# ScalarE's step functions in the second attention, moved behind the second head's turned probabilities and the values

## The reference

```
x = layernorm(x + L0_attn(x));  x = layernorm(x + L0_ffn(x))
x = layernorm(x + L1_attn(x));  x = layernorm(x + L1_ffn(x))
# L1_attn: causal attention, batch 4, 256 tokens, 32 heads of 128, with rotated
#          queries and keys (rope), plus a second, latent branch of 32 heads
# L1_ffn:  weights rounded to 16 levels (NF4) in blocks of 64 before their use:
absmax = max(|w|) per block;  idx = searchsorted(bounds, w / absmax)
w_used = NF4_CODE[idx] * absmax
```

## Time and profile before

| | |
|---|---|
| time, median of 3 runs (lowest, highest) | 2439.47 us (2437.63, 2440.76) |
| the profiled execution: its time; its span | 2439.4 us; 2437.5 us |
| busy in the span: PE, DVE, POOL, ACT | 2246.6, 1797.1, 1577.7, 1433.7 us |
| the second attention | about 805 to 2200 us of the span |
| one of its middle groups | about 173 us |

### The profile page before, as it was taken

How to read it: one execution, slowest core, us unless ns; L and a number is a source line. 1 busy time by engine, 2 the same in 40 slices (tenths; PEclk the granted TensorE clock), 3 DMA queues, 4 the chain that set the end, 5 groups by cost and what they waited for, 6 DMA issues and landing times. The chain is left out here.

```text
span 2437.5 us, 43787 instructions
## 1 busy us (share of the span) xinstructions
PE 2246.6 (92%) x14144; PEld 1993.3 (82%) x14144; DVE 1797.1 (74%) x3270; ACT 1433.7 (59%) x3947; POOL 1577.7 (65%) x1336
## 2 busy tenths in 40 slices
PE   7899999988998899998999999999999999987998
PEld 5788988876886788887888888888888888876886
DVE  5788777767533798888887888888888888964322
ACT  2657676652332567676676676776776766663232
POOL 3556657413444778778878878878788788752343
PEclk8999999988999999999999999999999999998999
DMA  3201111000001101101101111111111011004000
GB/s 101 63 27 42 59 32 43 11 18 1 1 1 55 56 25 54 54 13 61 51 25 50 47 33 51 39 42 50 40 40 52 31 50 40 19 5 146 1 18 18
DMA packets 49555, 95.38 MB, mean 39 GB/s; under 512 B 6768, under 2 KB 14224, under 8 KB 48976
## 3 DMA queue, kind: packets, MB, share of 16 engines
q1 hardware_dynamic: 49296, 92.24, 12.2%
HBM read 81.47 MB, written 10.75 MB: 38 GB/s over the span
## 5 line engine op out<-in xcount | busy, mean ns | idle before, releaser
L1280 POOL TENSOR_TENSOR a_nf_acc<-a_nf_acc,a_nf_term 128x512 f32<-128x512 f32 (+1 forms) x416 | 592.4, 1424 | 142.6 <-ACT a_nf_term L1374 72.0
L1334 ACT ACTIVATE a_probs<-bank,a_dip 128x128 f32<-128x128 f32 (+1 forms) x512 | 208.7, 420 | 192.1 <-DVE a_dip L1615 192.1
L1343 ACT ACTIVATE a_probs<-a_probs,a_share 128x128 f32<-128x128 f32 (+1 forms) x512 | 192.4, 464 | 67.7 <-DVE a_share L1621 67.7
L1799 POOL TENSOR_TENSOR f_w_lo<-WGU,f_w_hi 128x512 fp32r<-128x512 f32 x88 | 112.7, 1302 | 175.0 <-ACT f_w_hi L1810 175.0
L1261 POOL TENSOR_TENSOR a_qk_lo<-a_straight,a_qk_hi 128x512 fp32r<-128x512 f32 (+1 forms) x160 | 193.4, 1211 | 41.3 <-ACT a_qk_hi L1320 41.3
L64 PE MATMUL bank<-a_wo_hi,a_ot_hi 128*128 128x512 f32 x512 | 212.3, 415 | 0.0
L1626 DVE TENSOR_TENSOR a_pt_lo<-bank,a_pt_hi 128x384 fp32r<-128x384 f32 x256 | 141.0, 551 | 91.1 <-ACT a_pt_hi L1351 90.4
L1320 ACT ACTIVATE a_qk_hi<-a_straight 128x512 fp32r<-128x512 f32 (+1 forms) x160 | 94.4, 590 | 184.3 <-DVE a_straight L1600 184.3
L66 PE MATMUL bank<-a_wo_hi,a_ot_lo 128*128 128x512 f32 x512 | 201.2, 393 | 0.0
L65 PE MATMUL bank<-a_wo_lo,a_ot_hi 128*128 128x512 f32 x512 | 200.9, 392 | 0.0
L1685 DVE TENSOR_SCALAR a_nf_term<-a_nf_unit 128x512 f32<-128x512 f32 (+1 forms) x288 | 193.5, 716 | 3.4 <-DVE a_nf_unit L1668 0.6
(11 more groups left out here) (242 smaller groups left out, 8468.0 us busy)
## 6 DMA issues: line engine op xcount, KB each, us to landing
a_raw<-in_l_o SPq DMA_DIRECT2D x64, 256.0 KB, 2.8
a_raw<-in_l_vk SPq DMA_DIRECT2D x32, 384.0 KB, 3.1
a_raw<-in_l_ql SPq DMA_DIRECT2D x32, 320.0 KB, 2.9
a_raw<-in_l_ou SPq DMA_DIRECT2D x32, 288.0 KB, 2.8
a_raw<-in_l_nr SPq DMA_DIRECT2D x16, 384.0 KB, 3.1
a_nf_raw<-in_w_nf SPq DMA_DIRECT2D x24, 256.0 KB, 2.6
coded_w<-a_nf_acc SPq DMA_DIRECT2D x24, 256.0 KB, 2.0
f_codes<-coded_w SPq DMA_DIRECT2D x6, 512.0 KB, 3.9
```

Source lines behind the costliest of these rows:

```text
L1280: pool.tensor_tensor(acc, left, nf_term[:, i % CODE_RING, 0:w], ALU.add).then_inc(nf_added, 1)
L1334: act.activation(probs[:, n % 2, col:col + keys], bank[:, at:at + keys], ACT.Exp, bias=dip[:, n % 2, i:i + 1], accum_out=total[:, n % 2, i ...
L1343: ins = act.activation(cell, cell, ACT.Copy, scale=share[:, n % 2, i:i + 1])
L1799: pool.tensor_tensor(lo, src, hi.bitcast(F32), ALU.subtract).then_inc(part_lo[i], 1)
```

## The change

ACT's order within a step of the second attention: `code_terms(n)` goes behind `probs_high(n-1, 1)` and behind the high part of the values (VL), and stays ahead of the high parts of rotated queries (A) and keys (K). Nothing is computed differently, and no other engine's program is touched.

```diff
                     shares_applied(n)
-                    code_terms(n)
                     if not (first and n < 1):
                         probs_high(n - 1, 1)
-                    for name in l1_step_units(n, last):
-                        unit_high(name)
+                    units = l1_step_units(n, last)
+                    for name in units:
+                        if name[0] == "VL":
+                            plain_high(name)
+                    code_terms(n)
+                    for name in units:
+                        if name[0] != "VL":
+                            rope_high(name)
```

## The result

| | before | changed |
|---|---|---|
| median of 4 runs, us | 2440.09 | 2531.53 |
| range, us | 2437.63 to 2440.76 | 2529.29 to 2532.35 |
| profiled span, us | 2437.5 | 2530.5 |
| mean granted clock of TensorE | 0.969 | 0.954 |

The changed kernel takes 91.4 us more: the ratio is 1.0375, with a 95% interval of 1.0357 to 1.0393. The forecast was 2549, from 2485 to 2592.

A forecast was written before the change was run, and what follows sets the result against it. PE was taken to set the pace, busy 161.9 of 173 us in a middle group. Shifts of 76 us (56 within groups, 20 at passages) plus 33 us of clock on 2439.4 gave 2549 us, range 2485 to 2592.

The forecast's parts named there:

- The closed chain: PE's second turn, ACT's terms, POOL's sums, DVE's end and start of a piece, PE's second turn: closed, without slack.
- No slack, at the ends that do not look so: Read in step 8: L1648 starts at 1236.90, POOL's last sum ends at 1236.87, so a later sum delays it.
- Step 7 into 8: Piece's end in step 8: POOL's sum 2.2 us later behind the values' wait, taken as 2.0 us a group.
- Step 10 into 11: Piece's end in step 11, behind two VL: POOL's sum and PE's turn 4.5 us later in each group.
- the rival of half the shift: Sums run faster away from DVE's work, POOL has other gaps, the copies' lead helps: 2475 us, chance 10%.
- Step 11 into 0: Passage to the next group: sum 4.2 us later, POOL's gap in step 12 absorbs 1.3, leaving 2.9 us.
- Step 0 to 5: Piece's end in step 5: sum 1.8 us later, POOL's 1.30 us gap in step 1 takes most, leaving 0.5 us.
- The tail, costed at nothing: DVE's gain from copies 0.3 to 0.8 us sooner was costed at nothing, as given back at each piece's end.
- The clock: 22 falls at 1.5 us, 33 us: Behind longer PE stalls in steps 0, 5, 8 and 11: 22 additional falls to 1.2 GHz, 33 us, bounds nothing to 55.
- DVE's lead given back: DVE's waits for copies of turned probabilities and values halve, but at each piece's end it waits for POOL instead.
- Rotated queries with 0.4 us to spare: Rotated queries come 2 to 4 us later; tightest place, step 14, has some 0.4 us spare; charged nothing.
- the rival in which the clock holds: POOL's shift comes, but the low clock falls into the stalls and costs nothing: 2515 us, chance 17%.

The follow-up runs named there:

- The kernel with the clock kept: Changed kernel with zero-adding matmuls keeping PE busy ahead of the second turn in steps 0, 5, 8 and 11: 2495.74 us.
- its last link cut: Kernel before with DVE's L1648 moved to the end of steps 0, 5, 8 and 11: 2426.38 us; with the whole change added: 2438.76 us.
- the other order of DVE: Kernel before, DVE taking shares and first low halves ahead of a piece's end and start: 2500.83 us; with the change added: 2504.03 us.
- The run with the old order ahead of the ends: Changed kernel with ACT's old order kept in steps 0, 7, 10 and 11, new order in the others: 2458.35 us, ratio 1.0082 to the kernel before.
- The run with the new order in the tail alone: Kernel before with ACT's new order only in steps 12 to 15 of the last group: 2433.80 us, ratio 0.9972.

## Why the prediction was right, step by step

The kernel with the clock kept allows the sum to be read term by term, since its stretches hold the shifts and hardly any low clock. Differences to before, summed over the groups, in us:

| term | predicted shift | measured, clock kept | changed kernel, clock and all |
|---|---|---|---|
| step 5 to 8 | 16 | 15.7 | 21.1 |
| step 8 to 11 | 36 | 27.2 | 39.1 |
| step 11 to 0 | 20 | 18.7 | 25.3 |
| step 0 to 5 | 4 | 1.9 | 14.5 |
| tail | none | -5.4 | -8.3 |

*The closed chain.* Right, and the runs show it as the cause: with its last link cut, the change costs 12 us (3 on the other order of DVE). That it had no slack was read off two numbers that nearly met, the end of POOL's sum and the start of L1648; the list of waits did not name it. The new order in two steps alone cost 57 us; the forecast's two shifts are 8 × (2.0 + 4.5) = 52, and the stretches gave 45 with 11 from the clock.

*No slack, at the ends that do not look so.* The prediction read this in step 8 and took it for all ends. In steps 11 and 0 of the kernel before, L1648 starts 1.07 and 0.77 us behind POOL's last sum, and it is shorter:

```profile
1267.94 1.30 POOL L1280 TENSOR_TENSOR a_nf_acc<-a_nf_acc,a_nf_term 128x512 f32<-128x512 f32 x1 [0.18 <-POOL a_nf_acc L1280]
1269.19 1.30 POOL L1261 TENSOR_TENSOR a_qk_lo<-a_straight,a_qk_hi 128x512 fp32r<-128x512 f32 x1
...
1270.31 0.72 DVE L1648 SCALAR_TENSOR_TENSOR a_nf_acc<-a_nf_acc,a_nf_top 128x512 f32<-128x512 f32 x1
...
1152.61 1.28 POOL L1261 TENSOR_TENSOR a_qk_lo<-a_straight,a_qk_hi 128x512 fp32r<-128x512 f32 x1
...
1153.43 1.08 DVE L1648 SCALAR_TENSOR_TENSOR a_nf_acc<-a_nf_acc,a_nf_top 128x576 f32<-128x576 f32 x1
```

In step 11 it ends at 1271.03, in step 0 at 1154.51: 0.54 and 0.62 us behind the end of POOL's subtraction, as in step 8 (0.54). Gap and duration make 1.79, 1.85 and 1.79 us. So its end is tied to POOL's stream and not to its own start, and the later sum moves it by the full shift there too. In the changed kernel all 31 ends that wait start 0.02 to 0.04 us behind the sum and take 1.75 to 1.80 us. Without this, step 11's shift would have been a good us smaller. The prediction named the port and put its worth at a few tenths of a us at most. That these two ends have no slack it did not read from their rows, so there the forecast was right partly by luck.

*Step 7 into 8: 2.0 us.* Measured 34.67 - 32.83 = 1.84 in the groups in which the clock did not fall ahead of it. In the others it was 36.8, so 4.0.

*Step 10 into 11: 4.5 us, with a clock fall 6.0.* This is the term that was too big. Measured 3.8 with the clock kept (36.15 for 32.37 in a middle group; 27.2 over the eight groups), 4.0 in the middle groups with the new order in steps 7 and 10 alone, and 4.8 in the changed kernel with one low stretch. POOL's sum indeed waits for ACT (it starts at 1302.79), but the way behind it became shorter:

```profile
1300.27 0.44 ACT L1324 ACTIVATE a_vl_hi<-bank 128x320 fp32r<-128x320 f32 x1 [1.73 <-PE bank L66]
1300.60 1.32 ACT L1368 ACTIVATE a_nf_term<-a_nf_unit,a_edges 128x512 f32<-128x512 f32 x2
...
1302.79 1.30 POOL L1280 TENSOR_TENSOR a_nf_acc<-a_nf_acc,a_nf_term 128x512 f32<-128x512 f32 x1 [3.69 <-ACT a_nf_term L1374]
...
1305.58 1.77 DVE L1653 SCALAR_TENSOR_TENSOR a_nf_acc<-a_nf_acc,a_nf_top 128x512 f32<-128x512 f32 x1 [2.54 <-POOL a_nf_acc L1280]
```

The sum takes 1.30 us and not 1.62; DVE stands still beside most of it. From ACT's copy of the values to the sum's start it is 2.52 us, where the prediction had 0.44 + 2.21 = 2.65. Those are 0.45 us. The other 0.3 lie ahead of it: with the clock kept, PE ends the second VL 29.01 us behind the end of the piece in step 8 (1286.47 - 1257.46), and before 29.30 (1267.96 - 1238.66). The prediction took off such a gain of PE in step 7 and not here. The rival of half the shift had named the shorter sum, and was right on its sign.

*Step 11 into 0: 2.9 us.* Measured 18.7 / 7 = 2.7 with the clock kept. The gap of POOL that absorbs part of it was read rightly.

*Step 0 to 5: 0.5 us.* Measured 1.9 / 7 = 0.3 with the clock kept; with the clock and all 2.1. Nearly all of this stretch is the clock behind the stall of 5.9 us in step 0. The run with the old order ahead of the ends shows that the other steps are not free, though: steps 1 to 4 and the rest of the twelve were charged with nothing and cost 19 us there, the clock among them.

*The tail, costed at nothing.* This term was missing, and it is a gain of 8.3 us. The sentence that DVE gives its lead back at each piece's end is true of the groups, but behind the last end there is none to give it back at. The run with the new order in the tail alone shows it: -6.4 us in that stretch, and -6.3 between the medians of the time.

*The clock: 22 falls at 1.5 us, 33 us.* The size of one was right in the mean, 36 / 24 = 1.5, but not as a constant: 3.4 us of low clock cost 2.1 us in the stretch 5 to 8 (36.8 for 34.7) and 0.3 in the stretch 0 to 5 of the kernel before (51.55 for 51.3). Of the falls there were 29 - 11 = 18 more, which makes 27 us, and 29 us by their length (85.3 × 0.34). The two columns of the table differ by more, 92 - 58 = 34, since the kernel with the clock kept lacks falls of the kernel before as well. The stalls behind which it falls were forecast at 2.4, 3.5, 4.8 and 4.5 us in steps 5, 8, 11 and 0; they are 2.3 to 3.3, 3.2, 4.0 and 5.6 to 5.9 us in the middle groups. The Trainium skill, "TensorE: Matmul & The Clock Gate", section "HAM oscillation — how this bites in real kernels", says that work behind a long enough gap starts at half rate. The filled stalls show that this holds here as a cause, and not only beside the stall: the same late chain, with PE busy, was 36 us shorter.

*DVE's lead given back.* Right: its waits for the turned probabilities shrank from 90.4 to 37.7 us and for the values from 45.3 to 23.5, and its wait for POOL rose by 73.3.

*Rotated queries with 0.4 us to spare.* PE waits for their low halves now 6 times, 6.3 us in all, about the size of a wait of the loop that it takes the place of (9.4 us, 5 times, before). Charged with nothing, it was worth nothing that the stretches show.

*One thing that the sum did not hold.* In step 7 DVE's own terms became slower, beside a POOL that now runs its sums late and without a pause. DVE, then POOL, then three of DVE's terms at a time at which POOL stands idle:

```profile
1255.99 4.11 DVE L1690 TENSOR_SCALAR a_nf_term<-a_nf_unit 128x512 f32<-128x512 f32 x3
...
1255.70 1.28 POOL L1280 TENSOR_TENSOR a_nf_acc<-a_nf_acc,a_nf_term 128x512 f32<-128x512 f32 x1 [0.18 <-POOL a_nf_acc L1280]
1256.94 1.48 POOL L1261 TENSOR_TENSOR a_qk_lo<-a_straight,a_qk_hi 128x512 fp32r<-128x512 f32 x1
1258.37 1.45 POOL L1280 TENSOR_TENSOR a_nf_acc<-a_nf_acc,a_nf_term 128x512 f32<-128x512 f32 x1
...
1272.01 1.10 DVE L1690 TENSOR_SCALAR a_nf_term<-a_nf_unit 128x512 f32<-128x512 f32 x3
```

Three terms take 4.11 us, or 1.10 us. In the first case the second and third end at 1258.69 and 1260.10, 0.3 us behind one of POOL's instructions each (1258.42 and 1259.82). PE then has a new stall of 1.60 us ahead of the turn in step 7. Over the kernel the mean of DVE's 288 terms is 974 ns, for 716 before. It can't be the main cause: with the new order in steps 7 and 10 alone the terms take 689 ns, and 57 us are lost all the same. Its own price was not measured; of the 12 us that the change still costs with the piece's end last in its step, it may be a part (the terms take 1027 ns there, and 735 without the change). In the run with the old order ahead of the ends of pieces the terms take 941 ns, and it loses some 26 us ahead of the tail's gain, with the clock among them; that is an estimate of the most that they can cost.

**What the sum missed.** The forecast was +109, the result +91. The shifts were 64 us by the table, for 76, and 9 of the 12 us missing are step 10's term. The tail gave 5 to 8 us that were not in the sum. That leaves 33 to 36 us for the clock by the difference, 27 by the count of falls, for 33. So the mechanism, its four places and its last link were right; one term was a third larger than what was measured, and one gain was left out. The total alone would not decide this: 2531.5 lies midway between the forecast and the rival in which the clock holds, 2515. It is the count of low stretches and the 36 us that speak against that rival. A middle group takes 186 to 189 us by its stretches, where 184 to 188 was forecast.

## What to carry to other kernels

Before an instruction is moved behind a wait on an in-order engine, follow what it releases until the chain comes back to the engine that ends that wait. If it closes, and two neighbours on it end and start within hundredths of a us, expect to pay the delay nearly in full, whatever the waits that the move shortens, and the list of waits will not have shown it. A gap between the two is slack only if the second one's end, too, is free of the first engine's stream: compare its duration with and without the gap. If it must stay late, take the consumer's wait out of the way of what the bounding engine needs; put it behind all of that, not ahead of the next thing in the line. And don't price a stall by its length: compare the time between two fixed points on either side of it.

## What the runs showed of the hardware

- PE's long stalls are followed by the lower clock. Behind second turns that waited 3.26 and 3.99 us the granted clock was 0.54 and 0.55 for some 3 us, that is 1.2 GHz. Products of zeros in the stalls' place, 98 of 256 columns in a group (26 in 3.27 us in step 11), kept it at 2.4 GHz (1.00 over a middle group) and saved 36 us of 2532, though the engine was busy 10.7 us longer in such a group.
- A TENSOR_SCALAR of 128x512 in fp32 on DVE took 0.37 us with POOL idle and 1.37 us in the mean beside POOL's stream of two-operand instructions. The Trainium skill, "SBUF — State Buffer", section "SBUF: two separate sides", describes DVE and POOL as sharing a pair of ports by an exclusive lock, held for a whole instruction; the 4.11 us for three, beside three of POOL's, agree.
- L1648, which reads two tensors, took 1.76 us when it started with POOL's subtraction, and 0.72 us when it started 1.12 us behind it; both times it ended 0.54 us behind the end of POOL's instruction. Moved to the end of its step, its mean was 1.06 us.
